# Two steps of lead in place of four, and a later place for the transposed maxima

## The reference, cut to what matters

```
x = layernorm(x + attention(x))          # 8 batches, 1024 tokens, 256 channels, 16 heads of 16
x = layernorm(x + ffn(x))                # 256 -> 1024 -> 1024 -> 256, weights +1 and -1

qkv = x @ w_qkv.T + b_qkv
q, k = rope(elu(q) + 1), rope(elu(k) + 1)
attn = softmax(q @ k.T / 4) @ v  +  depthwise convolution of v over 3 tokens
h = relu(s0 * [x, -x] @ w0) * 2;  h = relu(s1 * h @ w1) * 2;  out = s2 * h @ w2
```

## Time and profile before

| | us |
|---|---|
| median of 3 runs | 2218.62 (2217.33 to 2225.1) |
| profiled execution, its own time | 2223.43 |
| its span | 2221.6 |
| TensorE busy | 2107.2 (95%) |
| VectorE busy | 1677.8 (76%) |
| ScalarE busy | 1493.0 (67%) |
| POOL busy | 914.7 (41%) |

### The profile page before, as it was taken

How to read it: one execution, slowest core, us unless ns; L and a number is a source line. 1 busy time by engine, 2 the same in 40 slices (tenths; PEclk the granted TensorE clock), 3 DMA queues, 4 the chain that set the end, 5 groups by cost and what they waited for, 6 DMA issues and landing times.

```text
span 2221.6 us, 43062 instructions
## 1 busy us (share of the span) xinstructions
PE 2107.2 (95%) x16896; PEld 846.8 (38%) x16896; DVE 1677.8 (76%) x3029; ACT 1493.0 (67%) x2865; POOL 914.7 (41%) x522
## 2 busy tenths in 40 slices
PE   4899999999999999999999999999999999999987
PEld 2123323334343434334343343434443343434344
DVE  7878889777787777877787777877778778787242
ACT  3288788666777667776777767776677766767531
POOL 1449249440776127570484407751185703300000
PEclk8599999999999999999999999999999999999999
DMA  5101110011010210102000110102101020000000
GB/s 178 28 16 35 55 45 16 28 37 56 10 33 8 78 34 15 35 27 77 16 16 27 53 59 8 35 9 72 39 16 33 22 65 16 11 13 20 1 20 19
DMA packets 40139, 76.85 MB, mean 35 GB/s; under 512 B 14992, under 2 KB 19456, under 8 KB 36864
## 3 DMA queue, kind: packets, MB, share of 16 engines
q1 hardware_dynamic: 34752, 51.02, 7.9%
q0 software_dynamic: 5184, 23.07, 2.8%
HBM read 46.27 MB, written 25.17 MB: 32 GB/s over the span
## 4 chain that ended last, share of the span: by engine, by line
PE 73%; DVE 12%; POOL 7%; ACT 3%; DMA 2%; issue 2%; SPq 1%; ACTq 0%; POOLq 0%; DVEq 0%
PE unit_banks L660 21%; PE unit_banks L545 19%; PE o_bank L590 17%; DVE maxima L911 8%; PE unit_banks L673 5%; PE unit_banks L617 4%; PE unit_banks L628 2%; ACT probs L749 2%; PE unit_banks L605 1%; DMA k_scratch<-parts 1%; PE unit_banks L555 1%; POOL work L1206 1%; POOL work L1207 1%; POOL parts L1224 1%; POOL parts L1223 1%
## 5 line engine op out<-in xcount | busy, mean ns | idle before, releaser
L911 DVE TENSOR_REDUCE maxima<-unit_banks 128x1 f32<-128x512 f32 x2048 | 1313.4, 685 | 397.5 <-PE unit_banks L545 391.5
L749 ACT ACTIVATE probs<-unit_banks 128x512 f32<-128x512 f32 x2048 | 1118.4, 597 | 594.3 <-PE unit_banks L555 588.5
L545 PE MATMUL unit_banks<-k_stack,q_stack 48*128 48x512 f16 x2048 | 665.0, 392 | 69.6 <-DVE maxima L911 30.6
L555 PE MATMUL unit_banks<-q_stack,k_stack 50*128 50x512 f16 x2048 | 652.8, 387 | 2.9 <-ACT probs L749 2.3
L590 PE MATMUL o_bank<-probs,v_pair 128*32 128x256 f32 x8192 | 566.2, 388 | 0.0
L660 PE MATMUL unit_banks<-h0T,w 128*128 128x512 f16 x2048 | 480.2, 380 | 0.0
L1234 POOL TENSOR_TENSOR attn<-o_rows_sb,rden 128x256 f32<-128x256 f32 x63 | 39.2, 623 | 905.4 <-DVE rden L924 894.3
L545 PEld LDWEIGHTS unit_banks<-k_stack,q_stack 48*128 48x128 f16 x2048 | 157.0, 94 | 608.7 <-DVE maxima L911 320.7
L590 PEld LDWEIGHTS o_bank<-probs,v_pair 128*32 128x32 f32 x8192 | 207.6, 109 | 296.6 <-issue 217.6
L660 PEld LDWEIGHTS unit_banks<-h0T,w 128*128 128x128 f16 x2048 | 188.9, 98 | 223.9 <-issue 34.2
L555 PEld LDWEIGHTS unit_banks<-q_stack,k_stack 50*128 50x128 f16 x2048 | 155.3, 93 | 21.0 <-ACT probs L749 13.9
(11 more groups left out here) (126 smaller groups left out, 1557.8 us busy)
## 6 DMA issues: line engine op xcount, KB each, us to landing
rows<-in_x POOLq DMA_DIRECT2D x8, 1024.0 KB, 5.2
xT_sb<-in_xT SPq DMA_DIRECT2D x8, 1024.0 KB, 14.1
q_stack<-q_scratch SPq DMA_DIRECT2D x128, 64.0 KB, 2.0
k_stack<-k_scratch SPq DMA_DIRECT2D x128, 64.0 KB, 2.0
out<-rows SPq DMA_DIRECT2D x8, 1024.0 KB, 4.0
q_scratch<-parts POOLq DMA_DIRECT2D x14, 512.0 KB, 3.3
k_scratch<-parts POOLq DMA_DIRECT2D x14, 512.0 KB, 3.3
q_stack<-q_scratch SPq DMA_DIRECT2D x128, 32.0 KB, 1.9
```

The lines of the kernel that those rows point to most:

```text
L545: nc.tensor.matmul(units.out(unit), q_stack[row:row + STACK, r, t * P:(t + 1) * P], k_stack[row:row + STACK, r, half * 512:(half + 1) * 51 ...
L555: nc.tensor.matmul(units.out(unit), k_stack[row:end, r, kt * P:(kt + 1) * P], q_stack[row:end, r, half * 512:(half + 1) * 512], start=True ...
L749: nc.scalar.activation(probs[:, 2 * (kt % 2) + h, half * 512:(half + 1) * 512], units.out(unit), ACT.Exp, scale=exp_regs[2 * (n % PAIRS) + ...
L911: nc.vector.reduce_max(maxima[:, v // T % 2, h * T + t, half:half + 1], units.out(unit), AXIS_X)\
```

## The change

It has three parts. LEAD is 2 in place of 4, so 10 tiles of scores stand ahead of step 0 in place of 12, the scores run 10 tiles ahead, and a pair's maxima are joined at the end of kt = 5 in place of kt = 3. The max rows go from kt = 5, ahead of the dense pieces, to kt = 6, behind them, and VectorE's split goes behind all other work between its two pairs of row maxima. And max rows have semaphores of their own. The line numbers of the changed file are 5 or 6 higher.

```diff
@@ -42,7 +42,7 @@
 STEPS = NB * PAIRS * T
 BATCH = PAIRS * T
 RING = 4
-LEAD = 4
+LEAD = 2
 BUFFERS = 3
 PARTS = 2
 ROWS = P // 2
@@ -62,7 +62,7 @@
 LN_OPS = 2 * T
 LOAD = 16 * 8
 
-O_ROWS_STEP, RECIPROCAL_STEP, MAX_ROWS_STEP = 2, 3, 5
+O_ROWS_STEP, RECIPROCAL_STEP, MAX_ROWS_STEP = 2, 3, 6
 
 Q_AT, V_AT = 6, 50
 K_AT, SCALE_AT = {1: 22}, ({}, {1: 28})
@@ -177,15 +177,19 @@
     units = []
     if kt == O_ROWS_STEP and n > 0:
         units.append(("O rows", n - 1))
-    if kt == MAX_ROWS_STEP and n + 1 < NB * PAIRS:
-        units.append(("max rows", n + 1))
     return units
+
+
+def max_rows_of(s):
+
+    n, kt = divmod(s, T)
+    return [("max rows", n + 1)] if kt == MAX_ROWS_STEP and n + 1 < NB * PAIRS else []
 
 
 HIDDEN = ("hT", "L0", "L1")
 READERS = {"S": ("scores", "scores"), "T": ("scores_T", "scores_T"), "proj": ("act", "act"),
            "hT": ("act", "dve"), "L0": ("act", "dve"), "L1": ("act", "dve"), "L2": ("dve", "dve"), "V": ("dve", "dve"),
-           "O rows": ("act", "act"), "max rows": ("dve", "dve"), "scale": ("dve", "dve")}
+           "O rows": ("act", "act"), "max rows": ("max rows", "max rows"), "scale": ("dve", "dve")}
 
 
 def program_order():
@@ -213,6 +217,8 @@
                     yield u, rings[""], True, True
                 for u, part in DEALT[s]:
                     yield u, rings[""], part == 0, ends_unit((u, part))
+                for u in max_rows_of(s):
+                    yield u, rings[""], True, True
     rings = (4, 5, 6, 0, 1, 2, 3)
     for u in [("O rows", NB * PAIRS - 1), *END_UNITS]:
         yield u, rings, True, True
@@ -372,9 +378,9 @@
 
 
         unit_full = {"scores": sem("scores_full"), "scores_T": sem("scores_T_full"),
-                     "act": sem("unit_full_for_act"), "dve": sem("unit_full_for_dve")}
+                     "act": sem("unit_full_for_act"), "dve": sem("unit_full_for_dve"), "max rows": sem("max_rows_full")}
         unit_free = {"scores": sem("scores_read"), "scores_T": sem("scores_T_read"),
-                     "act": sem("unit_read_by_act"), "dve": sem("unit_read_by_dve")}
+                     "act": sem("unit_read_by_act"), "dve": sem("unit_read_by_dve"), "max rows": sem("max_rows_read")}
         w_q_loaded = sem("w_q_loaded")
         w_kv_loaded = sem("w_kv_loaded")
         bias_loaded = sem("bias_loaded")
@@ -713,12 +719,11 @@
                 wait_stack(s + T + LEAD)
                 scores_both(s, 0)
                 for unit in own_units(s):
-                    if unit[0] == "O rows":
-                        o_rows(unit)
-                    else:
-                        max_rows_T(unit)
+                    o_rows(unit)
                 for unit, part in DEALT[s]:
                     dense(unit, part)
+                for unit in max_rows_of(s):
+                    max_rows_T(unit)
                 if s > 0 and not DEALT[s]:
                     weighted_v(s - 1, 0)
                     if kt == 0:
@@ -931,8 +936,8 @@
                 m = units.out(unit)[0:2 * T, 0:P]
                 nc.vector.tensor_scalar(max_rows[:, 0], m, -1.0 / MAX_ONES, None, ALU.mult).then_inc(max_split, 1)
                 dve.wait_ge(max_split, n + 1)
-                free(unit, nc.vector.scalar_tensor_tensor(max_rows[:, 1], m, -1.0 / MAX_ONES, max_rows[:, 0], ALU.mult,
-                                                          ALU.subtract))
+                nc.vector.scalar_tensor_tensor(max_rows[:, 1], m, -1.0 / MAX_ONES, max_rows[:, 0], ALU.mult,
+                                               ALU.subtract).then_inc(units.free_sem(unit), 1)
 
             def elu(c, ct):
 
@@ -1104,9 +1109,6 @@
                         row_max(v, 0, half)
                 for unit in done_behind(s - 1):
                     dense(unit)
-                for unit in own_units(s):
-                    if unit[0] == "max rows":
-                        split_max_rows(unit[1])
                 for w, at in enumerate((Q_AT, k_at(b + 1))):
                     if b + 1 < NB and i == at + 5:
                         join_sums(b + 1, w)
@@ -1129,6 +1131,8 @@
                     m = b - 1 - which
                     if m >= 0:
                         ln_moments(m, which)
+                for unit in max_rows_of(s):
+                    split_max_rows(unit[1])
                 if v < STEPS:
                     for half in range(2):
                         row_max(v, 1, half)
```

## The result

| | before | after |
|---|---|---|
| median of 7 runs each, us | 2219.42 | 2231.05 |
| lowest to highest | 2216.48 to 2225.10 | 2227.39 to 2240.66 |
| profiled execution, its own time | 2223.43 | 2240.66 |
| its span, mean granted clock | 2221.6, 0.978 | 2238.9, 0.976 |

The changed kernel is slower: ratio 1.0051, 95% interval 1.0035 to 1.0067, or 11.6 us by the medians. The profiled execution is the slowest of the seven; the other six took 2227.39 to 2233.16 at a mean granted clock of 0.981 to 0.984. So I take the prices of single steps from its timeline, and the total from the runs.

A forecast was written before the change was run, and what follows sets the result against it. It took the tight meshing of TensorE and VectorE, the second pair of row maxima having no slack, as the bound. Terms summed to 18.1 us: 2241.5 from the profiled 2223.43, 2236.7 less 4.8 for the clock; forecast 2237, range 2219 to 2247.

The forecast's parts named there:

- start: Before step 0: two tiles of scores fewer stand ahead, so it starts at 86.5 in place of 90.4, 3.9 us won.
- plain moves, 15 places: Steps 30, 62, 38, 54 of certain batches: moving kt = 5 to 6 delays the second row maxima, 0.30 each, 4.5 us.
- step 54, six: Step 54 of batches 1 to 6, behind an fp32 projection: the whole 0.42 delay counts, 2.5 us in all.
- step 6: Row maxima right behind statistics, VectorE without idle time: the split is paid in full, less 0.12; 3.1 us in all.
- step 14: Row maxima right behind the reading of an L1 unit: the split is paid in full, less 0.12; 2.7 us.
- ring, steps 21 to 24, seven: Step 23's second L0 unit gets a bank that VectorE reads later; with neighbouring steps 0.7 each, seven times, 4.9 us.
- batch 7, steps 45 and 46: Step 45 loses its bank wait and transpose, 0.9 won; step 46 costs 0.42; together minus 0.5 us.
- excess over the wait ahead of step 48: Steps 35 to 48: delays of 2.1 us a batch stay hidden until that wait is used up; 2.7 us show.
- late max rows in batch 0: Two empty steps leave too little time for the DMAs: rows land 0.4 late at four places, 2.0 us in all.
- land too late everywhere: Rival: slower DMAs beside other traffic cost up to 0.5 at some 50 places, 2255 us, if landing exceeds 4.5; chance 0.05.
- The clock: Behind waits ahead of step 48: two stretches at granted clock 0.50 go as the waits shrink, 4.8 us won.
- hidden: Rival: VectorE catches up its 0.42 in idle time, only banks and start remain, 2222 to 2229 us; chance 0.22.

The follow-up runs named there:

- E3: Changed kernel, but max rows take their turn in the ring of three banks ahead of the dense pieces, still computed behind them: 2232.27 us, 1.0043 of before.
- E9: Changed kernel with the max rows' ring turn ahead of dense pieces and their copy for step 48 ahead of SP's stack loads: 2217.86 us, 0.9980 of before.
- E5: Kernel before, with SP issuing the max rows for step 48 ahead of the stack loads that wait for POOL: 2208.82 us, 0.9935 of before.
- E6: Changed kernel, with SP issuing the max rows for step 48 ahead of the stack loads that wait for POOL: 2227.67 us, 1.0029 of before.
- E1: Changed kernel (LEAD 2, kt = 6) with the max rows ahead of the dense pieces again: 2225.09 us, 1.0021 of before.
- E12: E1 plus max rows for step 48 issued ahead of SP's stack loads, and two max-row DMAs in place of four: 2199.04 us, 0.9891 of before.
- E10: E5 plus two DMAs for the max rows in place of four: 2208.64 us, 0.9933 of before.
- E4: Changed kernel with the max rows copied by two DMAs in place of four: 2225.64 us, 1.0019 of before.
- E2: Changed kernel with LEAD 4 in place of 2: 2236.02 us, 1.0067 of before.
- E8: Kernel before with only semaphores of their own for the max rows: 2223.86 us, 1.0010 of before.
- E7: Kernel before with LEAD 3 alone, max rows still at kt = 5 ahead of the dense pieces: 2223.80 us, 1.0011 of before.

## Why the prediction was right, and where it was too high

**The direction and its reason.** The forecast was slower by 18.1 us against the profiled execution, 2237 in all; measured were 2231.05 and 11.6 by the medians. The steps that it named are those that grew. Set against the timeline of before, step by step, clock falls left out:

| term | forecast us | seen us |
|---|---|---|
| start | -3.9 | -3.8 |
| plain moves, 15 places | 4.5 | 2.9 (0.19 each) |
| step 54, six | 2.5 | 1.7 (0.29 each) |
| step 6 | 3.1 | 2.4 |
| step 14 | 2.7 | 2.4 |
| ring, steps 21 to 24, seven | 4.9 | 3.9 (0.56 each) |
| batch 7, steps 45 and 46 | -0.5 | -0.6 |
| excess over the wait ahead of step 48 | 2.7 | 2.3 |
| late max rows in batch 0 | 2.0 | 0.9 |
| sum (with 0.1 for the tail in the forecast) | 18.1 | 12.1 |

No term has the wrong sign. The mechanism held and its sizes were off, two of them above all. The late landing at step 40 of batch 0 is not in the table: what its wait of 1.73 us has above the 0.36 to 0.40 of the other places belongs to the rest named below.

**The plain move** was sized as 0.42 less 0.12 and measured 0.19: the step before loses 0.10, the step with the max rows gains 0.11, the next 0.18. The part that failed is "the transpose takes the place of the scores". It starts 0.1 ahead of that place and TensorE goes on to the scores after 0.21, so VectorE's lateness is shared out: part is the scores' own delay, which I had counted whole on VectorE. "Such steps last 4.35" is wrong with it; step 30 lasts 4.04. The same error is in step 54. It is not in step 6: there VectorE has no idle time, and batches 2 to 6 show 0.38 each, forecast 0.39. What that row lacks stands in batches 0 and 1, where three places at 0.25 were forecast and nearly nothing is seen.

**Batch 0.** The waits are there, 0.33 in the step with the max rows and 0.36 to 0.40 behind it. But the step behind a wait is 0.29 shorter. I took a late start as lost one to one; in batch 0 VectorE bounds, and TensorE, held up, finds its maxima already read. On the other side stands step 40 of batch 0, where the landing took 5.06 us and TensorE waited 1.73. The rival "land too late everywhere" came true at a few places only, and its limit of 4.5 was a little low: a landing of 4.65 ahead of step 56 of batch 6 cost nothing, one of 5.06 ahead of batch 4 made the step before it 0.19 longer than elsewhere.

**Steps 35 to 48** came as reckoned, step 40 at 1.36 (forecast 1.35) and step 47 at 0.95 (0.9), with step 46 at -0.68 in place of -0.35. E3 against E9 shows the point behind this term: the same edit is worth some 2 us with POOL's chain in the way and 10.9 without. E5 and E6 show it for the whole change: 11.6 us with the chain and 20.9 without it.

**The clock.** I had taken off 4.8 us for two falls behind waits ahead of step 48. They went, in steps 48 of batches 1 and 5 (1.64 and 2.94 us shorter). Others came in the profiled execution, in batch 0 and at step 40 of batch 2, which the forecast did not have. Its 17.2 us over the profiled execution of before are 12.1 of steps and 5.1 of clock and rest. In the other six runs the granted clock is higher than in before's profile. With the seen terms the forecast's own path, 2223.43 + 12.1 - 4.8, gives 2230.7, next to the median; that the difference between the runs is the clock alone is argued, not shown. That the forecast's two paths both gave 2236.7 was chance: the one from the median takes nothing off for the clock, and the 4.8 of the other equals the distance of the profiled execution from that median. Over all runs the changed kernel does have the higher clock, 0.982 against 0.980 of the runs of before beside the experiments, so the direction of that term was right; by the estimate of 1.7 us for each 0.001 it hides some 3 us of what the steps cost.

**Waits for row maxima** did not grow to 45 us (28.3). That step failed in how I expected the view to show it: the 0.2 of step 30 stands in the timeline as a longer distance between two scores and has no entry among the waits. The rival "hidden" had this for it, and its sum (only banks and start remain) is refuted by E9: with the turn of the ring undone, and nothing in front of step 48, the change still stands 10 us over E5 (0.9980 against 0.9935), start included.

**LEAD itself** is worth what the start shows only if nothing fixes a later point. Ahead of the dense pieces, with kt = 6, it costs 0.21% with the chain in place (E1) and wins 0.42% without it (E12 against E10). The two differ in more than the chain: E12 and E10 have two DMAs, E1 has four, and E4 puts the two at 7 us in the changed kernel. LEAD 2 with the swap and four DMAs was not run, so the chain's share alone is not shown.

## What to carry to other kernels

Where a chain on another engine fixes the start of a step, any gain before that point becomes a wait, and any loss is free until the wait is used up: read the distance from that chain's last DMA issue to the first use before pricing either, and take it out of the way first, here by issuing four small DMAs ahead of loads that wait for something else. A small unit in a shared ring of buffers costs by its turn more than by its work: find for each unit behind it who reads the buffer that it now gets, and when. Price a late instruction by what both engines do around it, since part of the delay is the other one's too.

## What I had not expected of the hardware

- Four DMAs of 2 KB landed 3.70 us after the first issue at most places, and 5.06 at one where POOL wrote 512 KB in between (issued 1.65 us behind the first). Other long ones in the changed kernel were 4.28, 4.41, 4.65 and 5.06 us. For the first place the write is the cause as far as six kernels can tell: where it is issued 1.15, 1.65 and 1.74 us behind the first of the four, they land at 4.59, 5.06 and 5.17 (E3, changed, E2), and where it comes 3.36 to 3.67 behind, they land at 3.70 (E6, E9, E1). The other four places have no such write beside them, and their cause stays open.
- The granted clock falls to 0.50 for 10.2 us behind a wait of 1.73, and not behind others as long: 2.21 ahead of step 48 of batch 1 in E1, 2.01 and 2.27 ahead of steps 48 of batches 1 and 5 in E8. As means over all runs, the kernels with long waits ahead of step 48 (before, E1, E3, E7, E8) have 0.978 to 0.980, and those without such a wait (E4 to E6, E9 to E12) 0.981 to 0.984. The changed kernel, with waits below 1 us there, has 0.982, and E2, with waits up to 1.35, has 0.980. That the waits make the difference is likely, not shown. From run to run of one kernel the mean granted clock scatters by 0.008 (0.976 to 0.984 in the changed kernel), and the time goes with it, by about 1.7 us for each 0.001 (2240.66 at 0.976 and 2227.39 at 0.984). In a kernel of such tightness this scatter is larger than most terms of the sum.
